# Score matmuls on two halves of TensorE's rows, and engine orders made by one list scheduler

## What is computed

```python
q = (LN(x) @ Wq.T), k = (ctx @ Wk.T), v = (ctx @ Wv.T)          # heads of 16
scores = q k' / 4;  masked keys and keys after the query: -inf
context = nan_to_num(softmax(scores)) @ v
x = x + (sigmoid(LN(x) @ Wg.T + bg) * context) @ Wo.T
scale = top 2 of softmax(LN(x) @ gate_w)                          # per expert and token
h_e = silu(scale_e * LN(x) @ w1_e) * (scale_e * LN(x) @ w3_e)
x = x + sum_e h_e @ w2_e
```

## Time and profile before

| what | us |
|---|---|
| runs: median, lowest, highest | 718.96, 718.38, 723.12 |
| span of the profiled execution | 718.9 |
| TensorE, VectorE, ScalarE busy | 653.6, 516.2, 386.0 |
| 63 to 103: maxima of chunk 0 | 40 |
| 103 to 532: maxima, scores, values | 429 |
| 532 to 569: scores and values | 37 |
| 569 to the end: experts, and the last chunk's router | 150 |

### The profile page before, as it was taken

One profiled execution on the slowest core, in us unless ns is written; L12 is line 12 of the kernel. 1 busy time (PEld: TensorE's weight loads), 2 busy tenths in 40 slices (PEclk: granted clock), 3 DMA queues, 4 the chain that ended last, 5 costly groups with the idle time before them and its releaser, 6 DMA issues.

```text
span 718.9 us, 11481 instructions
## 1 busy us (share of the span) xinstructions
PE 653.6 (91%) x4148; PEld 346.1 (48%) x4148; DVE 516.2 (72%) x1071; ACT 386.0 (54%) x762; POOL 68.8 (10%) x122
## 2 busy tenths in 40 slices
PE   5424989999989999999899999899998999999996
PEld 2313545546544345444333343333321388888885
DVE  4113888776897987787889788888944288777764
ACT  2210246664766675665867756567788633432331
POOL 3030440140001000220000000000000000000000
PEclk9775999999999999999999999899999999999999
DMA  9599697018001000039200130000000430607000
GB/s 297 90 136 131 109 127 78 3 36 98 2 2 19 2 1 1 2 74 160 77 1 1 45 74 1 1 1 2 1 2 1 67 52 1 133 17 140 6 31 30
DMA packets 36464, 36.87 MB, mean 51 GB/s; under 512 B 4471, under 2 KB 31447, under 8 KB 36408
## 3 DMA queue, kind: packets, MB, share of 16 engines
q1 hardware_dynamic: 33878, 33.65, 27.4%
q10 hardware_dynamic: 2530, 2.50, 1.1%
...
## 4 chain that ended last, share of the span: by engine, by line
PE 78%; DMA 9%; DVE 6%; ACT 3%; issue 2%; SPq 1%; POOL 1%; DVEq 0%; ACTq 0%; POOLq 0%
PE bank L1158 17%; PE ring L1118 15%; PE bank L1142 15%; PE ring L1219 4%; DMA qaug<-q_parts 4%; PE ring L1220 4%; PE ring L1221 4%; PE ring L1050 4%; PE bank L1050 4%; DVE pmax L892 3%; DMA q_parts<-stage 2%; PE bank L1236 2%; PE bank L1238 2%; PE bank L1237 2%; DMA k_parts<-stage 2%
## 5 line engine op out<-in xcount | busy, mean ns | idle before, releaser
L892 DVE TENSOR_REDUCE pmax<-ring 128x1 f32<-128x512 f32 (+4 forms) x640 | 333.1, 576 | 86.5 <-PE ring L1121 43.9
L769 ACT ACTIVATE probs<-bank 128x512 f32<-128x512 f32 (+4 forms) x592 | 286.7, 550 | 133.4 <-PE bank L1142 84.7
L1118 PE MATMUL ring<-kaug,qaug 97*128 97x512 bf16 (+4 forms) x640 | 201.9, 345 | 29.1 <-DMA qaug<-q_parts 23.3
L1142 PE MATMUL bank<-qaug,kaug 99*128 99x512 bf16 (+4 forms) x592 | 201.9, 357 | 6.4 <-ACT probs L769 5.5
L1158 PE MATMUL bank<-probs,vaug 128*32 128x512 f32 (+4 forms) x1184 | 143.2, 556 | 0.0
L1118 PEld LDWEIGHTS ring<-kaug,qaug 97*128 97x128 bf16 x640 | 61.3, 99 | 158.3 <-DVE pmax L892 82.2
L1142 PEld LDWEIGHTS bank<-qaug,kaug 99*128 99x128 bf16 (+1 forms) x592 | 57.2, 99 | 66.8 <-ACT probs L769 32.4
L796 ACT ACTIVATE u_sb<-u_sb 128x512 f32<-128x512 f32 x32 | 20.2, 632 | 59.2 <-DVE u_sb L1005 59.1
L1219 PE MATMUL ring<-x_hi,w_hi 128*128 128x512 f32 x128 | 50.4, 394 | 0.0
L1220 PE MATMUL ring<-x_lo,w_hi 128*128 128x512 f32 x128 | 50.2, 392 | 0.0
L1221 PE MATMUL ring<-x_hi,w_lo 128*128 128x512 f32 x128 | 49.8, 389 | 0.0
(11 more groups left out here) (110 smaller groups left out, 641.7 us busy)
## 6 DMA issues: line engine op xcount, KB each, us to landing
...
```

What stands on the lines that cost most here:

```text
L769: act.activation(probs[0:rows, u % NSLOT, h, off:CH], side_bank(e)[0:rows, off:CH], ACT.Exp, scale=DK ** -0.5).then_inc(side_read, 1)
L892: dve.tensor_reduce(pmax[:, n % 2, qt, h, slot:slot + 1], bank[:, 0:w], AX_X, ALU.max).then_inc(ring_read, 1)
L1118: last = pe.matmul(bank[:, b0:b1], qaug[0:ROW_MAX, c % 2, 4 * g + h, P * qt:P * (qt + 1)], kaug[0:ROW_MAX, 4 * g + h, k0 + b0:k0 + b1], st ...
L1142: last = pe.matmul(bank[0:r, off:CH], kaug[0:ROWS, 4 * g + h, P * j:P * j + r], qaug[0:ROWS, c % 2, 4 * g + h, off:CH], start=True, stop=n ...
```

## The change

- `kaug` and `qaug` are fp32r. A key or query has two parts, three products of 16 rows, one mask row, two maxima rows: 49 rows for `mx`, 51 for `st`. The even heads of each pair lie in partitions 0 to 63, the odd ones in 64 to 127, 8 pairs instead of 16 heads along the free dimension. A score matmul is so on one half of the array's rows.
- The triangle is added by two matmuls with 64 rows each, on the half of their head: for `mx` both over all its columns, for `st` 64 columns each.
- Parts are made in one step instead of three (L642 of the new kernel); for chunk 0 VectorE reads the bank itself. A reload is six transfers of 16 partitions as before, 8 heads x 512 x 4 B each.
- Banks 0 to 6 are one pool; at most 3 hold scores and 5 maxima. ScalarE instead of VectorE copies `m_row` and the router's turned scale; `m_row` is single, not double; a group's maxima leave in four transfers instead of two.
- The order of steps comes from a list scheduler in `make_plan`: ten streams, and at each turn the head that can start first by a model of TensorE's two row halves, the readers and the banks, ties by a deadline. SyncE and GpSimd run their steps by the model's times, not in the list's order.
- Pieces of 65 keys have 66 columns; of the pieces of a row block the four heads come next to each other. The maxima of a group may start once the fold before the last is planned.

TensorE from the second chunk's key projection on (before): the first maxima follow.

Four scores and two maxima stand between two value steps, drawn from all seven banks; a row names no half, but those of odd and even heads lie next to each other. Behind the last maximum stand 87 scores now and 63 before. The core of the diff:

```diff
-MAX_WIDTH = CH
-ST_BANKS = 3
...
-MASKED = -1.0e30
+MASKED = -(2.0 ** 99)
...
+PASS = 1 / 2.4
+READ_ACT, READ_DVE, SIGNAL, DRAIN = 50, 65, 30, 170
+RELOAD, SWITCH, HOP, LOAD = 100, 95, 2500, 15000
...
+SPREAD = 0.6
+TOLERANCE = 100
+MOST = {"st": 3, "mx": 5}
...
-Q_PARTS = (0, 0, 0, 1, 1, 2)
-K_PARTS = (0, 1, 2, 0, 1, 0)
+Q_PARTS = (0, 0, 1)
+K_PARTS = (0, 1, 0)
...
+    def start(e):
+
+        if e[0] in ("bn",) and norm not in (None, e[1:]):
+            return None
+        if any(d not in done for d in needs(e)):
+            return None
+        at = max([done[d] for d in needs(e)], default=0.0)
+        if e in due and seen < due[e] and e not in done:
+            return None
+        if not pe_time(e):
+            return at
+        if e[0] == "kq" and len(parts_out) >= 2:
+            at = max(at, parts_out[-2] - pe_time(e))
+        if e[0] in ("st", "mx"):
+            half = (e[4] if e[0] == "st" else max_pieces(e[1])[e[2]][1]) % 2
+            at = max(at, lane[half], last + 4)
+        else:
+            at = max(at, *lane)
+        if consumer(e):
+            at = max(at, min(bank_free[b] for b in banks(e)) + SIGNAL)
+        if e[0] in MOST:
+            held = sorted((bank_free[b] for b in range(7) if bank_user[b] and bank_user[b][0] == e[0]), reverse=True)
+            if len(held) >= MOST[e[0]]:
+                at = max(at, held[MOST[e[0]] - 1] + SIGNAL)
+        if column != (e[0] == "pv"):
+            at += SWITCH
+        return at
+
...
+        idle = at > max(last, *lane) + 1
+        end = at + pe_time(e) + (RELOAD if idle else 0)
+        if kind in ("st", "mx"):
+            half = (e[4] if kind == "st" else max_pieces(e[1])[e[2]][1]) % 2
+            end += 70 if kind == "st" and e[3] >= TPC * (e[2] // G) else 120 if kind == "mx" and max_pieces(e[1])[e[2]][4] else 0
+            lane[half] = end
+        else:
+            lane[0] = lane[1] = end
+        last, column = at, kind == "pv"
+        done[e] = end + DRAIN
+        engine = consumer(e)
+        if engine:
+            b = min(banks(e), key=lambda i: (bank_free[i], i))
+            places[e] = (b, bank_user[b])
+            if kind == "kq" and len(parts_out) >= 2:
+                free[engine] = max(free[engine], parts_out[-2])
+            free[engine] = max(free[engine], done[e] + SIGNAL) + read_time(e)
+            bank_free[b], bank_user[b] = free[engine] + 100, e
+            done[e] = bank_free[b] + LAG.get(kind, 0)
+        if kind == "y" and e[1:] == (0, 0):
+            places[e] = [bank_user[b] for b in Y_BANKS if bank_user[b]]
+        follow(e, at)
...
+    def deadline(name, e, at):
+
+        if name in ("scores", "maxima") and consumer(e) and e[0] != "mT":
+            return free[consumer(e)] - pe_time(e) - DRAIN
+        if name == "values" and e[0] == "pv":
+            more = sum(len(g) for g in streams["scores"] if g[0][1] <= e[1] + 1)
+            return free["act"] + more * 476 - pe_time(e) - 400
+        return first_at[e] + PATIENCE.get(name, 0)
+
+    feeding, first_at = False, {}
+    while any(streams.values()):
+        best = None
+        for name, stream in streams.items():
+            if not stream:
+                continue
+            heads = stream[0]
+            if name in ("scores", "maxima") and len(heads) > 1:
+                heads = [next((e for e in heads if half(e) == k), None) for k in range(2)]
+                heads = [e for e in heads if e]
+            for e in heads[:2]:
+                at = start(e)
+                if at is None:
+                    continue
+                at = max(at, last)
+                first_at.setdefault(e, at)
+                key = (max(0, round((at - last) / TOLERANCE)), deadline(name, e, at))
+                if best is None or key < best[0]:
+                    best = (key, name, e, at)
+        _, name, e, at = best
+        streams[name][0].remove(e)
+        if not streams[name][0]:
+            del streams[name][0]
+        if not streams["values"] and not feeding:
+            feeding = True
+        put(e, at)
+    return plan, units, places, {k: [e for _, _, e in sorted(v)] for k, v in others.items()}
...
-        qaug = sb("qaug", [P, 2, H, CH], BF16)
+        qaug = sb("qaug", [P, 2, HP, CH], F32R)
...
-            kaug = sb("kaug", [P, H, KP], BF16, attention)
+            kaug = sb("kaug", [P, HP, KP], F32R, attention)
...
-        m_row = sb("m_row", [8, 2, CH], BF16)
+        m_row = sb("m_row", [8, CH], F32R)
...
-            engine.tensor_tensor(left, left, parts[:, 0, 0:w], ALU.subtract).then_inc(rest_ready, 1)
-            engine.wait_ge(rest_ready, i + 1)
-            engine.tensor_copy(parts[:, 1, 0:w], left).then_inc(mid_ready, 1)
-            engine.wait_ge(mid_ready, i + 1)
-            engine.tensor_tensor(parts[:, 2, 0:w], left, parts[:, 1, 0:w], ALU.subtract).then_inc(lo_ready, 1)
...
+            return engine.tensor_tensor(parts[:, 1, 0:w], left, parts[:, 0, 0:w], ALU.subtract)
...
-            sp.dma_start(kaug[ROW_MASK:ROWS, :, :], ones_row.unsqueeze(1).to_broadcast([last_rows, H, KP])).then_inc(aug_k, 16)
-            sp.dma_start(qaug[ROW_MASK:ROWS, :, :, :].rearrange("p s h q -> p (s h) q"),
-                         ones_row[:, 0:CH].unsqueeze(1).to_broadcast([last_rows, 2 * H, CH])).then_inc(aug_q, 16)
-            for e in plan:
+            for half in range(2):
+                b = HALF * half
+                sp.dma_start(kaug[b + ROW_MASK:b + ROWS, :, :].bitcast(F32),
+                             ones_row.unsqueeze(1).to_broadcast([ROWS - ROW_MASK, HP, KP])).then_inc(aug_k, 16)
+                sp.dma_start(qaug[b + ROW_MASK:b + ROW_MAX, :, :, :].bitcast(F32).rearrange("p s h q -> p (s h) q"),
+                             ones_row[0:1, 0:CH].unsqueeze(1).to_broadcast([1, 2 * HP, CH])).then_inc(aug_q, 16)
+            for e in others["sp"]:
...
+                        for half in range(2):
+                            b = HALF * half + DK * r
+                            if what == "k":
+                                dst = kaug[b:b + DK, :, CH * c:CH * c + w]
+                                src = k_parts[K_PARTS[r], :, CH * c:CH * c + w]
+                            else:
+                                dst = qaug[b:b + DK, c % 2, :, :]
+                                src = q_parts[Q_PARTS[r], :, CH * c:CH * c + w]
+                            sp.dma_start(dst.bitcast(F32), src.rearrange("(h b d) q -> b d h q", b=2, d=DK)[half]
+                                         ).then_inc((k_landed if what == "k" else q_landed)[c], 16)
...
-                    for part in range(2):
-                        sp.dma_start(qaug[ROW_MAX + part:ROW_MAX + part + 1, c % 2, 4 * g:4 * g + 4, :],
-                                     m_row[4 * part:4 * part + 4, n % 2, :]).then_inc(m_landed[n % 4], 16)
+                    sp.wait_ge(*taken(e))
+                    for half in range(2):
+                        for part in range(2):
+                            row, at = HALF * half + ROW_MAX + part, 4 * half + GP * part
+                            sp.dma_start(qaug[row:row + 1, c % 2, GP * g:GP * (g + 1), :].bitcast(F32),
+                                         m_row[at:at + GP, :].bitcast(F32)).then_inc(m_landed[n % 4], 16)
...
+                elif kind == "mT":
+                    n = e[1]
+                    act.wait_ge(*made(e))
+                    if n:
+                        act.wait_ge(m_landed[(n - 1) % 4], 64 * ((n - 1) // 4 + 1))
+                    act.activation(m_row[:, :], bank_of(e)[0:8, 0:CH // 2].bitcast(BF16), ACT.Copy).then_inc(act_read, 1)
...
+                    hp, side = 2 * g + h // 2, h % 2
+                    b = HALF * side
+                    last = pe.matmul(bank[:, 0:w], qaug[b:b + ROW_MAX, c % 2, hp, P * qt:P * (qt + 1)],
+                                     kaug[b:b + ROW_MAX, hp, k0:k0 + w], start=True, stop=not diagonal)
+                    if diagonal:
+                        for a in range(2):
+                            last = pe.matmul(bank[:, d:w], eye_b[b:b + HALF, a + 1 - side, :],
+                                             tri_b[b:b + HALF, a + 1 - side, 0:w - d], start=False, stop=(a == 1))
+                    last.then_inc(dve_full, 1)
...
-                    last = pe.matmul(bank[0:r, off:CH], kaug[0:ROWS, 4 * g + h, P * j:P * j + r],
-                                     qaug[0:ROWS, c % 2, 4 * g + h, off:CH], start=True, stop=not diagonal)
+                    bank = make(e)
+                    last = pe.matmul(bank[0:r, off:CH], kaug[b:b + ROWS, hp, P * j:P * j + r],
+                                     qaug[b:b + ROWS, c % 2, hp, off:CH], start=True, stop=not diagonal)
                     if diagonal:
-                        last = pe.matmul(bank[0:r, off:off + P], tri_qk[:, 0:r], ident_b[:, :], start=False, stop=True)
-                    last.then_inc(side_full, 1)
+                        for a in range(2):
```

(4 more changed lines are left out.)

780 lines of the change are left out of this document (397 added, 383 removed).

## The result

Time after: 745.26 us median of 4 runs (734.51 to 746.96), beside 719.55 us for the kernel before on the same chip. The ratio is 1.026, with a 95% interval of 1.018 to 1.034: the change makes the kernel **slower by some 19 us**, where 664 was forecast. The ratio leaves out the two slowest of the four runs (746.65 and 746.96, at a granted clock of 0.90 against 0.92 in the fastest); the medians of all runs differ by 26 us. All four runs are slower than every run of the kernel before, but whether by 2% or more is not settled by four runs. The profiled execution is the fastest of them, with a span of 732.8 us.

A forecast was written before the change was run, and what follows sets the result against it. TensorE set the pace before; VectorE would after. First score at 106 us, plus 362 to the last maximum at 468, 45 to attention's end at 513, and 151 of experts: 664 us; own range 650 to 690, with rivals 638 to 712.

The forecast's parts named there:

- The head: Start of the program, a chain of transfers: first maximum at 70 us instead of 63, first score at 106.
- rival 3: Reloads run at twice the rate, up to 6.7 us less for each of four in the head: 639 us, chance 0.07.
- The ends: After the last maximum: 45 us to the end of attention at 513, then 151 us of experts.
- VectorE becomes the bound: Long stage from 106 us: VectorE's 348 us of work, 96% full, takes 362 us; TensorE needs only 324.
- the pair: Two 512-wide score matmuls on different row halves overlap and cost 0.23 us together, taking 100 us off TensorE.
- The changes of mode: Switching TensorE between row halves and full array: some sixty full-array items at 0.1 us each, 6 us, spare on TensorE.
- exist already: Score-to-value switches on TensorE, 148 each way at 0.09 us, stay as before and add nothing.
- The type: Score operands in fp32r, priced from the expert matmuls: 0.23 us for 512 columns, against 0.22 before.
- rival 2: TensorE, often waiting, runs 38% of the long stretch at half clock and needs 400 us: 702 us, chance 0.13.
- Rows behind reloads: Small transfers of row maxima wait behind reloads later in the queue, 13 us each, twice or three times: also 702 us.
- Rival 1: Score matmuls on the two row halves don't overlap, so the kernel is slower: 756 us, chance 0.08.
- Triangles: Each triangle becomes two matmuls on one half, 400 more: between 0 and 24 us of TensorE, taken as 12.

The follow-up runs named there:

- e13: Changed kernel with alternating halves, maxima rows ahead of two reloads and score operands read as bf16: 695.52 us, ratio 0.966 to the kernel before.
- e1: Computation left out, only rows of score-like matmuls on TensorE: a 512-wide pair on two halves takes 0.232 us in an unbroken row.
- e9: Computation left out, TensorE rows with value steps or triangles between scores: four scores and a value step take 1.66 us on halves, 1.96 as before.
- e2: Changed kernel whose planner delays a score matmul on the same half as the one before by 0.11 us: 727.66 us, ratio 1.003 to the kernel before.
- e6: Changed kernel with every score matmul on the full array instead of a half, still fp32r: 782.17 us, ratio 1.088 to the kernel before.
- e12: Changed kernel with score matmuls on the full array and operands read as bf16: 739.14 us, ratio 1.026 to the kernel before.
- e11: Changed kernel on halves, score operands read as bf16 from the upper two bytes: 710.96 us, ratio 0.990 to the kernel before.
- e7: Computation left out, TensorE runs stretches of some 50 us of one matmul kind without waits: clock fell to half on one half in fp32r.
- e4: Changed kernel with its 832 triangle matmuls left out: 730.3 us, ratio 1.014 to the kernel before.

## Why the prediction was wrong

- **The head was right.** First maximum at 70 forecast, 69.0 measured; first score at 106, measured 102.4, with TensorE idle before it for want of rows behind the query reload. The reloads kept their rate (13.6 to 14.8 us), so rival 3 was wrong.
- **The ends were nearly right.** From the last maximum (528.6) to the end of the last value step (579.8) 51 us against 45, and 153 from there against 151. Head and ends together are +5 to the forecast, the head's part being -4.
- **The step that failed** is "VectorE becomes the bound". VectorE's work, forecast as 348 us, was right (350); TensorE's in that stretch, 330 + 4 - 10 = 324, was not. TensorE was busy for 414 us and remained the bound. The long stage took 426 us, not 362: 64 of the 69 us by which the profiled execution misses the forecast. The rule that the prediction takes there from the Trainium skill's "TensorEngine Tiling (Array Packing)", PSUM Bottleneck, is worded weaker on the page: the copying out of PSUM "may become bottleneck". Only e13 comes near it.
- **Within it, the pair.** "So a 512-wide pair costs 0.23 us if two halves overlap wholly" is true of unbroken rows (e1). It was then applied to all 1105 score matmuls, though the kernel's rows break at every value step and full-array item, and though 195 of the 1097 that ran there had no partner. By the prices of e1 and e9: 195 x 0.115 = 22 us without partner; 97 value steps between scores x 0.12 = 12; 126 changes to and from full-array items x 0.15 = 19 (0.095 for each change, and the late start once for two), for which 6 were counted, 13 more. That makes 324 + 47 = 371 us of TensorE at full clock. This sum is an estimate from rows, and no run took its terms one by one but e2.
- **The changes of mode.** The 0.1 us counted for a full-array item among halves was right for one way: e1 measured 0.095. The count was wrong, since each such item is entered and left. That switches to the values "exist already" and add nothing was right as well (0.324 us on halves, 0.310 on the full array). The four scores saved 0.30 us instead of 0.42 because of the type. "TensorEngine Tiling (Array Packing)", Key Properties, in the Trainium skill says that switching the tiling mode drains the engine; the trace agrees with the 0.095 us.
- **The type** was a term of almost nothing (0.23 for 0.22). The stages measured it at 45 us on the full array (e6, e12) and at 27 us on halves (changed kernel, e11), and against bf16 without a step some 12 us more (an estimate). The rows of the expert matmuls had shown fp32r in an unbroken row with equal neighbours, and I took their start distance for a score among bf16 triangles and fp32 values. The term left out is the late start, 0.10 us behind each value step, triangle or full-array item.
- **The clock** (rival 2, 0.13) came true in part. Its sign was to be "a granted clock under 0.9 between 110 and 470"; it was 0.93 over the long stage, with 62 us at half. The 371 us at full clock become 371 + 62/2 = 402: the clock is the largest single term. Its reason was a waiting TensorE; but TensorE was busy, and e7 has a fall without any wait.
- **Rows behind reloads "again later in the queue"**, which rival 2 named, happened once: 6.5 us idle at 155 us. With it the sum is 408 of the 426 us; the last 18 stay open, between the type, the banks and the order.
- **Rival 1** (halves don't overlap, 756) was wrong in its mechanism: pairs start together, and e6, on the full array, took 782. It priced the type too low as well. Its sign, TensorE at 97% and VectorE under 80%, nearly came (97% and 82%), and by that sign alone one would have blamed the wrong cause.
- **Triangles.** 12 us were counted for their doubling. A triangle cost 0.08 us a score in e1 and 0.06 before, which for 400 is 8 us; leaving all of them out gave 9 us of the time (e4). The term was not where the forecast failed.

So the change gained 40 us by its halves and lost as much or more by the type of operands that the halves demand, since 97 rows of bf16 do not fit in 64. The half clock, 31 us of loss by estimate against 3 before, is counted in these sums and is more than the 13 us by which the stage became longer; what brings it on is open. The new order and queue cost little beside these.
